# Attention block, 8 heads on one core: row maxima brought into the score banks by ScalarE and VectorE instead of by a fourth matmul

## The reference

```python
# x: (4, 512, 48, 48) fp32, so B=4, C=512, T=2304; 32 groups, 8 heads of 64 channels
mean = xg.mean(axis=(2, 3), keepdims=True)          # group norm
var = xg.var(axis=(2, 3), keepdims=True)
xn = (xg - mean) * jax.lax.rsqrt(var + EPS)
xn = xn.reshape(b, c, T) * gn_w[None, :, None] + gn_b[None, :, None]
qkv = jnp.einsum('oc,bct->bot', qkv_w, xn) + qkv_b[None, :, None]
qkv = qkv.reshape(b * N_HEADS, 3 * ch, T)
q, k, v = jnp.split(qkv, 3, axis=1)
scale = 1.0 / math.sqrt(math.sqrt(ch))
weight = jnp.einsum('bct,bcs->bts', q * scale, k * scale)
weight = jax.nn.softmax(weight.astype(jnp.float32), axis=-1)
a = jnp.einsum('bts,bcs->bct', weight, v).reshape(b, c, T)
hout = jnp.einsum('oc,bct->bot', proj_w, a) + proj_b[None, :, None]
return (xn + hout).reshape(b, c, h, w)
```

## Time and profile before

| | us |
|---|---|
| median of 3 runs | 4159.61 (4155.93 to 4160.69) |
| profiled execution | 4164.19 |
| its span, first to last instruction | 4162.4 |

### The profile page before, as it was taken

How to read it: one execution, slowest core, us unless ns; L and a number is a source line. 1 busy time by engine, 2 the same in 40 slices (tenths; PEclk the granted TensorE clock), 3 DMA queues, 4 the chain that set the end, 5 groups by cost and what they waited for, 6 DMA issues and landing times.

```text
span 4162.4 us, 86380 instructions
## 1 busy us (share of the span) xinstructions
PE 4034.5 (97%) x33648; PEld 2660.7 (64%) x33648; DVE 2285.1 (55%) x2982; ACT 1723.8 (41%) x2487; POOL 3009.8 (72%) x1641
## 2 busy tenths in 40 slices
PE   6999999999899999999989999999999999999997
PEld 4666666656766666665676656666567666666666
DVE  4555555574455555556545555556654555555553
ACT  2443444454344444445334444444543444444443
POOL 0777778777378787777737877877773877777793
PEclk9999999999999999999999999999999999999999
DMA  2000000020400000012040000001103000000004
GB/s 69 8 8 12 8 10 12 29 80 10 142 8 10 10 10 10 10 41 67 12 140 10 10 8 10 12 8 57 53 25 124 12 8 10 10 10 7 7 7 141
DMA packets 116464, 128.16 MB, mean 31 GB/s; under 512 B 56080, under 2 KB 105808, under 8 KB 115536
## 3 DMA queue, kind: packets, MB, share of 16 engines
q1 hardware_dynamic: 116048, 122.49, 9.4%
HBM read 84.43 MB, written 37.75 MB: 29 GB/s over the span
## 4 chain that ended last, share of the span: by engine, by line
PE 85%; DVE 4%; issue 3%; DMA 3%; POOL 3%; SPq 0%; ACT 0%; DVEq 0%; POOLq 0%; ACTq 0%
PE scores L532 26%; PE oacc L550 25%; PE pool_bank L476 12%; PE aux_banks L498 11%; PE pool_bank L488 6%; POOL denom L1057 3%; DVE maxima L842 2%; PE scores L631 2%; PE pool_bank L519 1%; DMA att_in<-att 1%; DMA out<-probs 1%; DVE recip L917 1%; PE pool_bank L504 1%; PE scores L476 1%; DVE probs L991 0%
## 5 line engine op out<-in xcount | busy, mean ns | idle before, releaser
L1057 POOL TENSOR_TENSOR denom<-denom,probs 128x768 f32<-128x768 f32 x1536 | 2834.5, 1845 | 652.6 <-ACT probs L743 552.8
L842 DVE TENSOR_REDUCE maxima<-aux_banks 128x2 f32<-128x768 f32 x1728 | 1656.9, 959 | 1432.4 <-PE aux_banks L498 1430.1
L743 ACT ACTIVATE probs<-scores 128x768 f32<-128x768 f32 x1728 | 1308.2, 809 | 1602.0 <-PE scores L532 1155.0
L550 PE MATMUL oacc<-probs,vals 128*64 128x384 f32 x6912 | 1303.0, 492 | 0.0
L550 PEld LDWEIGHTS oacc<-probs,vals 128*64 128x64 f32 x6912 | 505.3, 137 | 475.4 <-issue 438.3
L498 PE MATMUL aux_banks<-k_hi,q_hi 64*128 64x384 f32 x3456 | 692.3, 394 | 54.8 <-DVE maxima L842 47.0
L498 PEld LDWEIGHTS aux_banks<-k_hi,q_hi 64*128 64x128 f32 x3456 | 329.5, 184 | 599.1 <-issue 409.2
L532 PE MATMUL scores<-q_hi,k_lo 64*128 64x384 f32 x3456 | 593.0, 335 | 0.0
L532 PE MATMUL scores<-q_hi,k_hi 64*128 64x384 f32 x3456 | 589.7, 335 | 2.7 <-ACT probs L743 2.7
L532 PE MATMUL scores<-q_lo,k_hi 64*128 64x384 f32 x3456 | 591.4, 334 | 0.0
L532 PE MATMUL scores<-max_row,one_rows 64*128 64x384 f32 x3456 | 590.7, 334 | 0.0
(11 more groups left out here) (94 smaller groups left out, 1590.9 us busy)
## 6 DMA issues: line engine op xcount, KB each, us to landing
xtile<-x SPq DMA_DIRECT2D x72, 384.0 KB, 3.2
att<-o_norm SPq DMA_DIRECT2D x96, 192.0 KB, 1.9
att_in<-att SPq DMA_DIRECT2D x24, 768.0 KB, 6.4
probs<-x SPq DMA_DIRECT2D x24, 768.0 KB, 4.6
out<-probs SPq DMA_DIRECT2D x24, 768.0 KB, 5.5
xn<-x SPq DMA_DIRECT2D x4, 1152.0 KB, 8.6
wk<-wqkv_t SPq DMA_DIRECT2D x32, 128.0 KB, 2.4
wq<-wqkv_t SPq DMA_DIRECT2D x32, 128.0 KB, 2.4
```

Of the source, the lines that this page charges most:

```text
L550: ins = mm(oacc[head(e), 0:N], vals[p % 2][:, kt, head(e)], prob(s)[:, e * N:(e + 1) * N], start=(kt == 0), stop=(kt == KT - 1))
L743: a(prob(s).rearrange("p (h n) -> p h n", n=N), scores[:, s % 2, :, 0:N], ACT.Exp, scale=SCALE).then_inc(probs_ready, 1)
L842: v.tensor_reduce(maxima[:, :, qt, kc], aux_banks[:, :, 0:N], AX.X, ALU.max).then_inc(aux_done, 1)
L1057: gp.tensor_tensor(acc, acc, prob(s), ALU.add).then_inc(added, 1)
```

## The change

The fourth product goes, with `one_rows`, `max_row`, `row_parts`, the identity and the transposition. A step's pair of score banks is written with the negated maxima before its three products, which now all add onto what is there (`start=False`). This writing is called a seed. ACT writes the seeds of even steps, DVE those of odd steps, each a copy of 128x768 fp32 from SBUF to PSUM out of `seeds`, which holds the negated maxima of 384 queries of both heads on all 128 partitions; there are two such buffers, for even and odd blocks. A seed waits for the exponential that read the bank before. `seeds` is filled by SP: it sends `neg_max` (128x6) to DRAM so that the numbers of a head lie in a row (768 pieces of 4 bytes), waits for that, and reads the row back onto all 128 partitions. Once, before the first step, `open_banks` runs four matmuls into the score banks. `SPREAD`, which deals the quarters of the three projections of a block over its slots, has the same twelve quarters in another order.

```diff
-    SPREAD = (((0, 0, 2), (1, 2, 4)), ((3, 0, 1), (4, 1, 3), (5, 3, 4)), ((7, 0, 2), (8, 2, 4)))
+    SPREAD = (((0, 0, 2), (1, 2, 4)), ((3, 0, 1), (4, 1, 2), (5, 2, 4)), ((6, 0, 1), (7, 1, 2), (8, 2, 4)))
...
+            def send_max(n, blk):
+                par = blk % 2
+                sp.wait_ge(neg_ready, n + 1)
+                sp.dma_start(neg_rows.rearrange("r q -> q r"), neg_max[:, :],
+                             allow_slow_non_contiguous=True).then_inc(neg_out, 16)
+                sp.wait_ge(neg_out, 16 * (n + 1))
+                if not isinstance(n, int) or n >= 2:
+                    for slot in range(2):
+                        sp.wait_ge(seeded[slot], PRIMED + KT // 2 * (n - 1))
+                sp.dma_start(seeds[par][:, :], neg_rows.rearrange("r q -> (r q)").partition_broadcast(128))\
+                  .then_inc(seeds_in[par], 16)
...
-            def max_rows(n, u):
-                pe.wait_ge(neg_ready, n)
-                filled(mm(bank_for(u)[0:D, 0:128], neg_max[:, :], ident[:, :], start=True, stop=True), u)
...
+            def make_scores(s, b):
                 p, j, kt = s // STEPS, s % STEPS // KT, s % KT
-                if product == 0 and s >= 2:
-                    pe.wait_ge(probs_ready, PROBS_PRIMED + BSTEPS * b + s - 1)
-                elif product == 3 and kt == 0:
-                    pe.wait_ge(max_row_in, 32 * (BLOCKS * b + p * CH + j + 1))
-                ks, qs = ((k_hi[p % 2], q_hi), (k_lo[p % 2], q_hi), (k_hi[p % 2], q_lo), (one_rows, max_row))[product]
...
+                pe.wait_ge(seeded[s % 2], PRIMED + BSTEPS // 2 * b + s // 2 + 1)
+                for n, (ks, qs) in enumerate(((k_hi[p % 2], q_hi), (k_lo[p % 2], q_hi), (k_hi[p % 2], q_lo))):
+                    for e in range(2):
+                        last = mm(scores[:, s % 2, e, 0:N], ks[head(e), keys], qs[head(e), chunk(j)],
+                                  start=False, stop=(n == 2), skip_group_check=True)
+                last.then_inc(scores_full, 1)
...
+            def seed(s, b):                      # ScalarE, even steps
+                blk = s // KT
+                if s % KT < 2:
+                    act.wait_ge(seeds_in[blk % 2], 16 * (BLOCKS // 2 * b + blk // 2 + 1))
+                if s < 2:
+                    act.wait_ge(banks_opened, 1)
+                    act.wait_ge(proj_saved, PRIMED + PJ * b)
+                else:
+                    act.wait_ge(probs_ready, PROBS_PRIMED + BSTEPS * b + s - 1)
+                a(scores[:, s % 2, :, 0:N], seeds[blk % 2].rearrange("p (e n) -> p e n", n=N), ACT.Copy)\
+                    .then_inc(seeded[s % 2], 1)
...
             def stream(b, last):                 # ScalarE
                 before, after = PLANS[last]
+                seed(0, b)
                 for i in range(PAIRS * SLOTS):
                     for s in range(GS * i, GS * i + GS):
                         exponentials(s, b)
+                    if GS * i + 2 < BSTEPS:
+                        seed(GS * i + 2, b)
...
+            def seed(s, b):                      # VectorE, odd steps; the waits are the same
+                v.tensor_copy(scores[:, s % 2, :, 0:N], seeds[blk % 2].rearrange("p (e n) -> p e n", n=N))\
+                    .then_inc(seeded[s % 2], 1)
...
             def stream(b, last):                 # VectorE
                 for i in range(PAIRS * SLOTS):
                     for s in range(GS * i, GS * i + GS):
                         unit_of_step(s, b, last)
...
+                    if GS * i + 3 < BSTEPS:
+                        seed(GS * i + 3, b)
                     for key in completed(before[i]):
                         behind(key, b, last)
```

More of the change, by code:

```diff
@@ L95, in batch_plan @@
                     whole(before, s0 + s, key)
-            for j in range(1, CH):
-                whole(before, s0 + maxrow_slot(j), ("maxrow", p, j))
-            if p < PAIRS - 1 or more_batches:
-                whole(before, s0 + SLOTS + maxrow_slot(0), ("maxrow", p + 1, 0))
             for j in range(CH):
@@ L160, in unit_at, with ends_block, block_of @@
         return u // STEPS, u % STEPS // CH, u % CH
+    neg_rows = nc.dram_tensor("neg_rows", (2 * QT, 128), fp32, kind="Internal").ap()
+    def ends_block(unit):
+        _, qt, kc = unit
+        return kc == CH - 1 and qt % QT == QT - 1
+    def block_of(unit):
+        p, qt, _ = unit
+        return p * CH + qt // QT
     with ExitStack() as ctx:
@@ L267, in attention_block_program @@
         neg_ready = sem("neg_ready")
-        max_row_in = sem("max_row_in")
+        neg_out = sem("neg_out")
+        seeds_in = [sem(f"seeds_in{i}") for i in range(2)]
+        banks_opened = sem("banks_opened")
+        seeded = [sem(f"seeded{i}") for i in range(2)]
         scores_full = sem("scores_full")
@@ L375, in stream @@
                         load_x(nb, XITEMS + n + XPARTS)
+                    unit = unit_at(s, last)
+                    if unit is not None and ends_block(unit):
+                        blk = block_of(unit)
+                        send_max(BLOCKS * b + blk, blk)
                     if s in PUT_AT:
@@ L452, in _ @@
             sp.wait_ge(att_out, PRIMED + 16 * BLOCKS * B)
-            sp.wait_ge(max_row_in, 32 * BLOCKS * B)
+            for par in range(2):
+                sp.wait_ge(seeds_in[par], 16 * BLOCKS // 2 * B)
             for signal in (wq_in, wk_in, wv_in):
```

102 lines of the change are left out of this document (35 added, 67 removed).

## The result

The changed kernel takes **4341.59 us** (median of 4 runs, 4335.83 to 4352.18), the kernel before 4160.15 beside it: ratio **1.0441 [1.0419, 1.0463]**. It is slower by 181 us, where 4131 was forecast; it lies outside the range. The profiled execution took 4335.83, its span is 4334.0 against 4162.4, and the mean granted clock 0.970 of full speed against 0.991.

What follows compares the result with a forecast made beforehand. PE, 97% busy, was taken to set the time. Inner blocks -54, last pairs +4 and +18, batch beginnings +3 give -29: from 4164.2 to 4135, or 4131 allowing for the profiled run's 4.6 above the median; range 4050 to 4220.

Steps and rivals of the forecast that it cites:

- Fourth product and transposition: On PE: dropping the product takes off 302 us (864 slots by two by 0.175), the transposition 20 us.
- the handshake: On PE: aux2 waits for DVE's reduction, until 1.49 after aux1; 0.16 of new waiting, so a slot gains 0.09.
- the 0.10 of a wait: On PE: a wait of aux2 costs 0.10 us beyond its length, its weights not being loaded beside the product before.
- Both seeds: Copies into score banks: ACT's lasts about 0.82 us, hidden, cost 0; DVE's about 0.96 us.
- GpSimd's rival: DVE's seed takes turns with POOL's adds: at least 4240 us; 8%.
- The failed step: slot 5: DVE in slot 5: o_norm at 3.93, free at 5.81, reduction 0.74 late, so aux2 of slot 6 goes at 2.23.
- The DMAs: Maxima to seeds by two DMAs in series: 3.6 us for 768 pieces, 8.3 in all, hidden within 12.5.
- The rival: Late maxima: 768 pieces take 9.2 us, the chain 13.9, every block waits 1.4, total 4265; 5%.
- P: Theory of the experiments: o_norm on DVE and GpSimd's adds lock each other out; the new phase makes DVE the loser.
- The clock: Rival: slot 6's longer wait lowers PE's granted clock, 1.2 us in each of 72 inner blocks, total 4217; 6%.
- Last pairs: Mostly empty slots where DVE has more to do: 4 us more in the last batch, 18 in the other three.
- D: Theory of the experiments: the first DMA of the maxima is late.

Runs made afterwards that it cites:

- b_no4_pool: The kernel before without its fourth product (maxima computed, not subtracted) and with o_norm on GpSimd: 4076.25 us, ratio 0.9805.
- a_half: a_pool_quick with each reduction taken over half of its columns, 384 instead of 768: 3875.38 us, ratio 0.9321.
- a_pool_quick: The changed kernel with o_norm on GpSimd and maxima written as 128 pieces of 24 bytes, in wrong order: 4103.26 us, ratio 0.9871.
- b_norm_pool: The kernel before with o_norm on GpSimd and nothing else: 4141.61 us, ratio 0.9963.
- a_pool_lead: The changed kernel, complete, with o_norm on GpSimd and AHEAD = KT + 8 for KT + 6: 4108.68 us, ratio 0.9883.
- a_rows_quick: The changed kernel, o_norm left on DVE, maxima written as 128 pieces of 24 bytes, in wrong order: 4302.77 us, ratio 1.0344.

## Why the prediction was wrong, point by point

- **Fourth product and transposition, the handshake, the 0.10 of a wait.** Right. Slots of 4.60, 3.96 and 3.31 against 4.59, 3.94 and 3.30; b_no4_pool and a_half bear them out from both sides.
- **Both seeds.** Right, 0.95 and 0.82. GpSimd's rival was wrong in its place: the seed, with one input in SBUF, keeps 949 ns on average beside the adds.
- **The failed step: slot 5.** The prediction put `o_norm` at the distances of the rows of before ("`o_norm` 3.93", 0.56 long) and so took its length as its own. It depends on when it starts against an add. With a product less before them, the exponentials and so the adds moved 0.18 forward (the second add from 4.06 after aux1 to 3.88), `o_norm` only 0.08 (from 4.03 to 3.95). The add now starts just ahead of it, and it lasts 2.17. That made slot 6 6.28 and not 4.68, and brought on the seed's lateness and the clock's falls in the inner blocks. Taken out, 147 us go. The trace of before gave the means to see it: an `o_norm` at 1509.52 beside adds, and two adds that took 0.4 too long. The prediction's own shift of 0.175 for the exponentials, taken on to the adds, puts the second one at 3.88, ahead of its own 3.93 for `o_norm`. The Trainium skill, "SBUF — State Buffer", section "Who interferes with whom", says that a DVE instruction with two SBUF inputs contends with a GpSimd instruction that reads SBUF, and that for the two-port modes whoever issues first keeps the shared pair for the whole instruction. The traces agree: 0.56 or 2.17 us for DVE, 1.82 or 2.22 for the add, according to who comes first. I had weighed that page for the new instruction and not for the old one that the change moves in time.
- **The DMAs.** The second failed term: 3.6 us for 768 pieces, worked out from 512 pieces in 2.4, and measured 9.7 (median, from its issue to the issue of the DMA that waits for it). The rival had this number (9.2) and 5% of the chance; its price of 134 us was too high. Beside P it is 39 us, since the slower blocks give it time; with P gone it is 91 (4194.59 to 4103.26). The weights go in longer runs from DRAM (128 KB in 512 pieces); these are single floats, one to a piece.
- **The clock.** The mechanism was named (1.2 us a slot; 1.5 measured), and rejected because slot 6 would wait only 0.9. It waits 1.48 and 0.58. The clock is a consequence here: with both causes gone no inner slot 6 has it, and the mean is 0.986. No run isolates its share. An estimate from the trace: the 25 inner slots 6 with a lower clock are some 43 us longer than their like at the full clock, nearly half of the 95 of the inner blocks.
- **Last pairs.** +22 forecast. Where P and D are gone, a last pair of the first three batches takes 248 to 250 us (a_pool_quick), against 242 in b_norm_pool, and in the last batch the two are equal within 1 (201.2, 201.8): about +20. Right in the sum; of the 4 for the last batch nothing is seen, but `o_norm` is not on VectorE there.
- **Sum.** -29 was forecast for a change that leaves `o_norm` and the seeds alone. With both held so, a_pool_lead less b_norm_pool is -33 and a_pool_quick less b_norm_pool is -38. That is not quite like for like, since it also takes out the lateness that `o_norm` gives slot 6. The like case is the last batch of a_rows_quick: its inner blocks are 0.75 and 0.99 shorter than in the same batch of the kernel before, where 0.70 and 0.84 were forecast. The step-by-step sum of PE was sound; what it left out was the state of engines off the path. One slip lies in its range: the bounds named there, added up, give 4026 to 4190 and not 4060 to 4185, which changes nothing here.

## What to carry to other kernels

When a change shifts the phase of one engine against another, list every instruction, old ones too, that shares something with a neighbour (here a VectorE product of two SBUF tensors beside GpSimd's adds) and look for unlike durations of the same instruction in the trace of before: a min and a max of 0.56 and 2.0, or an add of 2.2 among 1.8, is a hidden lock that may turn round. A product taken off TensorE brings little when each unit waits for a reduction: shorten the handshake first (228 us here, in a run that reduces only half of the columns), and check that a filled wait doesn't come back at the next unit. A DMA is priced by its pieces, from a row with pieces of that size, not by its bytes or by longer runs.
